# The second attention's value product, written clip by clip and normalised in one instruction

## The reference

```python
def _L0_ffn_ref(x, W_qkv, b_qkv, W_gate, b_gate, A, B_lora, W_proj, b_proj):
    ...                                        # b = 128 clips, s = 46 tokens, d = 192
    qkv = qkv_base + sparse_out.reshape(b, s, 3 * d)
    qkv = qkv.reshape(b, s, 3, H, head_dim).transpose(2, 0, 3, 1, 4)     # H = 12, head_dim = 16
    q, k, v = (qkv[0], qkv[1], qkv[2])
    attn = jax.nn.softmax(jnp.einsum('bhqd,bhkd->bhqk', q, k) * scale, axis=-1)
    out = jnp.einsum('bhqk,bhkd->bhqd', attn, v)      # the product that changes
    out = out.transpose(0, 2, 1, 3).reshape(b, s, d)
    return out @ W_proj.T + b_proj
    ...
h = _L0_tok_ref(x, L0_tok_W, L0_tok_b)
h = h + _L0_attn_ref(_layernorm(h, axis=-1), L0_attn_Wq, L0_attn_Wk, L0_attn_Wv)
h = h + _L0_ffn_ref(_layernorm(h, axis=-1), ...)
```

## Time and profile before

| | |
|---|---|
| median of the timed runs | 631.47 us (630.83 to 632.0) |
| the profiled execution's own time | 629.51 us |
| its span on the engines | 627.8 us |
| TensorE busy | 577.8 us (92%), 7811 matmuls |
| VectorE busy | 497.5 us (79%) |
| GpSimd busy | 382.3 us (61%) |
| ScalarE busy | 356.1 us (57%) |
| mean granted TensorE clock | 0.965 |

### The profile page before, as it was taken

The page is one execution under the profiler, slowest core; times in us unless marked ns, Lnnn a source line. Parts: engine busy times, 40 slices in busy tenths (PEclk is TensorE's granted clock), DMA queues, the critical chain, the costliest instruction groups (busy, mean ns, idle before and its releaser), DMA issues.

```text
span 627.8 us, 20585 instructions
## 1 busy us (share of the span) xinstructions
PE 577.8 (92%) x7811; PEld 520.6 (83%) x7811; DVE 497.5 (79%) x1312; ACT 356.1 (57%) x688; POOL 382.3 (61%) x646
## 2 busy tenths in 40 slices
PE   1879879999999999999999999999999999997784
PEld 1767768888898989998999999898989898776674
DVE  6523665678888888888898989898888889998774
ACT  3637536666666575657666666666665545543431
POOL 7684887987767677677676867677676633221010
PEclk9979889999999999999999999999999999998965
DMA  8795546887675776767677768575867160615511
GB/s 196 175 209 91 132 96 149 147 193 134 166 150 134 147 169 133 171 129 162 137 164 153 165 142 173 131 155 146 157 142 135 34 127 25 131 37 95 103 28 36
DMA packets 60132, 83.15 MB, mean 132 GB/s; under 512 B 11754, under 2 KB 44087, under 8 KB 58499
## 3 DMA queue, kind: packets, MB, share of 16 engines
q1 hardware_dynamic: 60035, 81.85, 61.2%
HBM read 50.24 MB, written 13.57 MB: 102 GB/s over the span
## 4 chain that ended last, share of the span: by engine, by line
PE 79%; DMA 8%; DVE 7%; ACT 2%; issue 2%; SPq 2%; DVEq 0%; ACTq 0%
PE ps_r L1436 24%; PE ps_tok L1428 7%; PE ps_tok L1429 6%; PE ps_tok L1430 6%; PE ps_p L1688 5%; PE ps_s L1675 4%; PE ps_r L1428 4%; PE ps_r L1430 4%; PE ps_r L1429 4%; DMA k<-qk_scratch 3%; PE ps_r L1589 3%; DMA v<-L_tok_W 2%; PE ps_r L1718 2%; PE ps_r L1526 2%; DMA qk_scratch<-qk 1%
## 5 line engine op out<-in xcount | busy, mean ns | idle before, releaser
L730 POOL TENSOR_TENSOR xs<-raw,xs 90x368 f16<-90x368 f32 x188 | 162.5, 888 | 40.7 <-ACT xs L824 40.7
L1428 PE MATMUL ps_tok<-w_tok,xs 128*128 128x192 f16 x576 | 145.3, 252 | 4.0 <-DVE h L1203 1.5
L1429 PE MATMUL ps_tok<-w_tok,xs 128*128 128x192 f16 x576 | 144.3, 250 | 0.0
L1430 PE MATMUL ps_tok<-w_tok,xs 128*128 128x192 f16 x576 | 144.2, 250 | 0.0
L824 ACT ACTIVATE p2T<-ps_p 128x552 f16<-128x552 f32 x64 | 40.2, 628 | 64.0 <-PE ps_p L1688 44.0
L824 ACT ACTIVATE xs<-raw 90x736 f16<-90x736 f32 x96 | 76.4, 805 | 0.0
L1428 PEld LDWEIGHTS ps_tok<-w_tok,xs 128*128 128x128 f16 x576 | 66.2, 115 | 7.5 <-POOL xe L730 2.6
L730 POOL TENSOR_TENSOR xe<-raw,xe 90x368 f16<-90x368 f32 x64 | 55.4, 884 | 23.4 <-ACT xe L824 23.4
L1429 PEld LDWEIGHTS ps_tok<-w_tok,xs 128*128 128x128 f16 x576 | 66.8, 116 | 1.0
L1430 PEld LDWEIGHTS ps_tok<-w_tok,xs 128*128 128x128 f16 x576 | 66.2, 115 | 0.2
L957 ACT ACTIVATE qk<-ps_r,b_qk 128x368 f16<-128x368 f32 x48 | 27.2, 567 | 47.3 <-PE ps_r L1430 47.3
(11 more groups left out here) (178 smaller groups left out, 1594.8 us busy)
## 6 DMA issues: line engine op xcount, KB each, us to landing
raw<-x SPq DMA_DIRECT2D x32, 1035.0 KB, 7.7
qk_scratch<-qk SPq DMA_DIRECT2D x32, 276.0 KB, 2.8
q<-qk_scratch SPq DMA_DIRECT2D x48, 138.0 KB, 4.8
k<-qk_scratch SPq DMA_DIRECT2D x48, 138.0 KB, 5.6
xs<-xe SPq DMA_DIRECT2D x30, 184.0 KB
v<-v2s SPq DMA_DIRECT2D x64, 76.5 KB, 6.4
out<-h2b SPq DMA_DIRECT2D x16, 240.0 KB
xs<-xe SPq DMA_DIRECT2D x15, 149.5 KB
```

Source lines behind the costliest of these rows:

```text
L730: nc.gpsimd.tensor_tensor(lo, src, hi, ALU.subtract).then_inc(s_lo, 1)
L1428: mm(dst, stat[0], mov[0], start=start, stop=False)
L1429: mm(dst, stat[0], mov[1], start=False, stop=False)
L1430: return mm(dst, stat[1], mov[0], start=False, stop=stop)
```

## The change

The product is written clip by clip. For each head pair and each clip there is one `split_product` with 64 stationary columns (that clip's slot of queries) and 34 moving columns (that clip's values). Its output is the clip's own 64 rows, and both clips' results stand in the same 204 columns of the bank. The unused cross products are gone. With both clips in the same columns, `norm2` reads them with one multiply of 110 rows by 192 columns. The rows between the clips (46 to 63) are now read as well, so the unused query columns of `p2T`'s high part are set to one at the start, which keeps the reciprocal there finite. Semaphore counts follow: `s_o2` counts one per pair and not two, `s_wz` one more.

```diff
-                 "pv0": (s_o2, 8, 2), "pv1": (s_o2, 8, 4), "pv2": (s_o2, 8, 6), "pv3": (s_o2, 8, 8),
+                 "pv0": (s_o2, 4, 1), "pv1": (s_o2, 4, 2), "pv2": (s_o2, 4, 3), "pv3": (s_o2, 4, 4),
...
-                            sp.wait_ge(s_wz, 6)
+                            sp.wait_ge(s_wz, 7)
...
-                        act.wait_ge(s_wz, 4)
+                        act.wait_ge(s_wz, 5)
...
             def clear_rooms():
                 nc.vector.memset(f32_of(p2T[:]), 0.0).then_inc(s_wz, 1)
+                dve.wait_ge(s_wz, 4)
+                nc.vector.memset(p2T[:, 0].rearrange("p a (b q) -> p (a b) q", q=SLOT)[:, :, NT:SLOT], 1.0).then_inc(s_wz, 1)
                 nc.vector.memset(v2_room, 0.0).then_inc(s_wz, 1)
...
-                        pv = bank(f"pv{p}")[:, 0:HEADS * 2 * (HD + 1)].rearrange("p (b h e) -> p b h e", b=2, e=HD + 1)
-                        nc.vector.reciprocal(rc[0:ROWS, p, :], pv[0:ROWS, 0, :, HD]).then_inc(s_rc, 1)
+                        pv = bank(f"pv{p}")[:, 0:HEADS * (HD + 1)].rearrange("p (h e) -> p h e", e=HD + 1)
+                        nc.vector.reciprocal(rc[0:ROWS, p, :], pv[0:ROWS, :, HD]).then_inc(s_rc, 1)
                         dve.wait_ge(s_rc, g * PAIRS + (p + 1))
                         dve.wait_ge(s_o2z, 1)
-                        for b in range(2):
-                            r = slice(SLOT * b, SLOT * b + NT)
-                            nc.vector.tensor_tensor(o2[r, p, 0:D].rearrange("p (h e) -> p h e", h=HEADS), pv[r, b, :, 0:HD],
-                                                    rc[r, p, :].unsqueeze(2).to_broadcast([NT, HEADS, HD]),
-                                                    ALU.mult).then_inc(s_o2, 1)
+                        nc.vector.tensor_tensor(o2[0:ROWS, p, 0:D].rearrange("p (h e) -> p h e", h=HEADS), pv[0:ROWS, :, 0:HD],
+                                                rc[0:ROWS, p, :].unsqueeze(2).to_broadcast([ROWS, HEADS, HD]),
+                                                ALU.mult).then_inc(s_o2, 1)
...
-                        dst = bank(f"pv{p}")[:, 0:2 * HEADS * (HD + 1)].rearrange("p (b h e) -> p b h e", b=2, e=HD + 1)
+                        dst = bank(f"pv{p}")[:, 0:HEADS * (HD + 1)].rearrange("p (h e) -> p h e", e=HD + 1)
                         for j in range(HEADS // 2):
-                            last = split_product(dst[:, :, 2 * j:2 * j + 2, :],
-                                                 [p2T[:, part, j, :] for part in range(2)],
-                                                 [v2[:, g % 2, :, :, p, j, part, :] for part in range(2)], True, True)
+                            for b in range(2):
+                                rows = slice(SLOT * b, SLOT * (b + 1))
+                                last = split_product(dst[rows, 2 * j:2 * j + 2, :],
+                                                     [p2T[:, part, j, rows] for part in range(2)],
+                                                     [v2[:, g % 2, b, :, p, j, part, :] for part in range(2)], True, True)
```

More of the change, by code:

```diff
@@ L978, in o2_twin @@
                     if g is not None:
-                        act.wait_ge(s_o2, g * 8 + 8)
+                        act.wait_ge(s_o2, g * 4 + 4)
                         copy(o2[:, :, D:2 * DA], o2[:, :, DA:D]).then_inc(s_o2d, 1)
@@ L1712, in ot @@
                         if kh == 0:
-                            pe.wait_ge(s_o2, g * 8 + 8)
+                            pe.wait_ge(s_o2, g * 4 + 4)
                         else:
```

## The result

The changed kernel takes 645.93 us (median of 4 runs, 642.34 to 648.4) against 631.67 us (4 runs, 630.83 to 632.0): a ratio of 1.0249, with a 95% interval of 1.0196 to 1.0302. The forecast was 652 us, in a range of 641 to 668. Slower is right, and the reason for it (a halved array, entered and left 64 times) too; the price of the product itself was put too high.

What follows compares the result with a forecast made beforehand. TensorE was taken to bound the kernel, 79% of the chain and full from 190 to 520 us. 629.5 + 47 x 0.43 (20.2) = 649.7 us profiled, other terms zero; median 2.0 higher: 652 us, range 641 to 668.

Steps and rivals of the forecast that it cites:

- Steps within one half: In `pv`, each half starts a matmul once in 32 ns, set by the load of 64 stationary columns.
- the rival built on it: Loads in `pv` at half the speed seen in `s_`: 670 to 680 us, chance 0.05.
- The order: In `pv`, threes start in program order, only the change of half is cheap: 0.81 us from first to last start.
- The bounds named beside it: Body of 35 steps in `pv`: 0.57 us if halves overlapped throughout, 1.12 us if they never did.
- only going in and out is paid: Rival: halves interleave in `pv`, load hidden; 0.78 us, +0.19 each, 640 us in all; chance 0.11.
- Going in and out: Around each `pv`, the array empties when it goes from whole to halved and back: 0.09 us more each way.
- The sum per `pv`: Entry, body and exit of one `pv`: 1.02 us against 0.59, so 0.43 us more.
- `norm2` is worth nothing where TensorE is full: Up to 522 us, the saved multiply, 0.38 us a pair, lies beside a TensorE that never waits: no gain.
- The tail nets to zero: Behind 522 us, up to 2.7 us gained in `norm2` against 2.7 lost in `pv`: zero, bounds -2.7 to +5.
- The rest at nothing: Extra clearing at 84 us (0 to +0.7), renumbered waits, bank freeing and fetching 1152 more matmuls: taken as 0 us.
- No overlap: Rival: halves never overlap in `pv`; 1.33 us, +0.74 each, 666 us in all; chance 0.17.
- Not slower: Rival: 128 filled rows don't empty the array, `pv` stays 0.59 us; 629 to 631 us, chance 0.05.

Runs made afterwards that it cites:

- sixes: Changed kernel with the matmuls reordered: two head pairs of clip 0, then the same two of clip 1; 646.58 us, ratio 1.0247.
- eighteens: Changed kernel with its two loops exchanged: all 18 matmuls of clip 0, then all 18 of clip 1; 672.7 us, ratio 1.0677.
- the run with one multiply: Kernel before with the single multiply of 110 rows, product left at full width, clip 1's output left out; 629.69 us, ratio 0.9969.
- the one with two: Changed kernel with two multiplies of 46 rows in place of one of 110; 645.97 us, ratio 1.0234.
- alternating variant: Changed kernel with the clips alternating from matmul to matmul, as `s_` does; 647.22 us, ratio 1.0272.
- halves of 68: Kernel before, each product cut by its stationary side: 36 matmuls of 64 stationary, 68 moving columns, two multiplies kept; 645.03 us, ratio 1.0222.

## Why the prediction was right, and where it was not

*Steps within one half: 32 ns, right.* It was taken from pairs of `s_`, with 48 rows and 46 moving columns. It held for 128 rows and 34 columns, and for 68; only the first step in a half is longer, 52 ns. That the load is what sets it stays argued. The rule of the Trainium skill ("TensorE: Matmul & The Clock Gate", on LDWEIGHTS) by which such a load takes 53 ns did not come true at the full clock, nor did the rival built on it (670 to 680 us).

*The order: wrong, and this is the step that failed.* "Matmuls start in order, so inside a three there are two full steps of 32 ns" gave 0.81 us from first to last start; 0.57 is what the trace has. The halves overlap although the program has threes, since TensorE looks past up to three waiting matmuls for one that can go to the free half (the sixes and the eighteens). The rows of `s_` could not tell, because strict alternation looks the same either way, and so the order was an assumption and not a reading. The bounds named beside it, 0.57 and 1.12, were the right ones, and the first has come true: the body is that of the rival "only going in and out is paid". The Trainium skill ("TensorE: Matmul & The Clock Gate", Part 3 on packing small matmuls) has matmuls strictly in program order in start and end. For starts, this case's traces disagree: clip 1's first start comes 10 ns behind clip 0's first in the changed kernel, 6 ns behind its third in the sixes and 6 ns behind its 15th in clip after clip, each time ahead of matmuls that stand before it in the program.

*Going in and out: right, and not complete.* 0.09 and 0.09 us were forecast, 0.093 and 0.085 measured. Left out was the longer first step of the next stage, about 0.025 us. It could have been read: the step behind the first full-width matmul was not looked at when `s_` was.

*The sum per `pv`: 0.43 forecast, 0.218 measured.* The body gives 0.015 instead of 0.25 (0.81 less the 0.56 of before), the ends 0.18 as forecast, the next stage about 0.025. Over the 47 `pv` that is 10.2 us instead of 20.2.

*`norm2` is worth nothing where TensorE is full: right*, by the run with one multiply (33.26 us a group) and the one with two (34.13, as changed). *The tail nets to zero: not refuted, and no more.* It became 0.3 us longer, with 17 `pv` in it that are each slower; of seven pairs of multiplies on the chain one multiply is left. But this is one execution of either kernel: with 36 matmuls in two halves as well, the tail is 3.3 us longer than the changed kernel's in the alternating variant, which has the single multiply, and only 0.4 us longer in the one with halves of 68, which has two.

*The rest at nothing: wrong by 1 to 2 us.* That "in `s_` 24 with their loads are fed in 0.37 us" was true for one stage, and said nothing on a supply that has to last over the program. The waits without releaser are 1.6 us that no term held.

Against the profiled execution: 649.7 forecast, 644.3 measured. The `pv` took 10.0 us off, the idle time of TensorE put 1.6 back, the head 2.3, the tail 0.3 and the unassigned part of the middle 0.6; that makes -5.2 of -5.4. So the forecast came close partly by luck: the head's accident and the waits, 3.9 us, gave back over a third of what the failed step had put too high. The rival with the right body said 640 us, and missed by as much on the other side.

*Rivals.* "No overlap" (666 us) fell with the pairs. "Not slower" fell at the place it named: the step ahead of the first `pv` matmul is 0.17 us, not 0.08. A product that fills all 128 rows pays for the halved array all the same.

## What to carry to other kernels

Before a full-width product is cut into two column halves between full-width neighbours, put down 0.2 us for each visit to the halved array, and ask how much work a visit holds: here the work itself stayed the same, 0.57 us against 0.56, and the 47 visits up to the end of the full stretch lost 10 of the 14 us. Cutting the moving columns of a half from 68 to 34 gained 0.03 us for 36 matmuls, since something else sets its pace. If both halves are used, their matmuls should alternate in blocks of no more than three. Work saved on an engine that stands beside a full one is worth at most what it saves outside that stretch: 25 us less on VectorE (472.4 against 497.5, in the run with one multiply) brought about 2 us by the runs here, and none that the profiled execution shows.

## What the runs showed of the hardware that was not expected

- Matmuls for one column half start ahead of up to three waiting ones of the other: 36 in 0.57 us in threes, 0.65 in sixes, 1.03 in eighteens.
- At full width and 34 moving columns, starts come 25.4 ns apart on average. Between halves they come at 3 ns (ones), 6 ns (sixes, eighteens) and 10 ns (threes). Within a half it is 32 ns, with 34 and with 68 moving columns, and 52 ns for the first step.
- A visit to the halved array costs 0.093 us in, 0.085 out and about 0.025 in the next step. The change is paid between two halved shapes too: `s_` (48 rows) and `pv` (128 rows) follow each other directly at three places in the changed kernel's tail at the full clock, and 114 or 115 ns lie between the last start and the first, as much as on the way out to full width (0.12).
- TensorE waited up to 2.1 us without a releaser in programs with many short matmuls, and each of the 12 waits ended 1.35 to 1.54 us behind the landing of a packet of instructions. That the one causes the other was not tested.
